# Banded attention: output projection behind the scores, first mask ahead of the residual add, and mask, scale and minimum of a head in one VectorE pass

## The reference

```python
q, k, v = jnp.split(shift_token(x) @ wqkv, 3, axis=-1)      # 8 heads of 64 each
q, k = l2norm(q) * qs, l2norm(k) * ksc
q, k = rotary_xpos(q, k)
...
bq = q.reshape(b, h, w, WINDOW, d) * QK_SCALE               # WINDOW = 64, QK_SCALE = 8
sim = jnp.einsum('bhwid,bhwjd->bhwij', bq, bk)              # own and previous window
mask = (i < j) | (i > j + WINDOW) | (j == -1)
sim = jnp.where(mask, -jnp.finfo(sim.dtype).max, sim)
attn = jax.nn.softmax(sim, axis=-1)
out = jnp.einsum('bhwij,bhwjd->bhwid', attn, bv)
...
x = x + o @ wo
```

## Time and profile before

| | |
|---|---|
| median of 3 runs | 3254.89 us (3253.47 to 3256.94) |
| the profiled execution | 3241.83 us |
| its span, first to last instruction | 3239.8 us |
| mean granted clock of TensorE | 0.893 of full speed |
| busy, share of the span | TensorE 79%, VectorE 60%, ScalarE 48%, GpSimd 25% |
| the four passes, twelve steps of each | 123.2 to 123.5 us each |

### The profile page before, as it was taken

The page is one execution under the profiler, slowest core; times in us unless marked ns, Lnnn a source line. Parts: engine busy times, 40 slices in busy tenths (PEclk is TensorE's granted clock), DMA queues, the critical chain, the costliest instruction groups (busy, mean ns, idle before and its releaser), DMA issues. The chain is left out here.

```text
span 3239.8 us, 44443 instructions
## 1 busy us (share of the span) xinstructions
PE 2552.5 (79%) x15874; PEld 1765.7 (55%) x15874; DVE 1949.3 (60%) x3314; ACT 1567.2 (48%) x3740; POOL 822.1 (25%) x598
## 2 busy tenths in 40 slices
PE   7999987787787778777688888664576888789987
PEld 4555554544543544543577777241242765769877
DVE  5666667747846866756444343335556898475554
ACT  4444446746744764755312121644353765156651
POOL 0000004514502532520235353000000776014500
PEclk9999998989989999998799999787797999687896
DMA  1000001000102000000000000000000222000010
GB/s 38 10 10 10 16 31 39 21 18 16 24 5 66 16 16 20 17 14 18 1 0 0 0 0 0 3 10 7 5 12 28 72 72 93 2 9 1 2 55 14
DMA packets 24921, 63.93 MB, mean 20 GB/s; under 512 B 3217, under 2 KB 9873, under 8 KB 23729
## 3 DMA queue, kind: packets, MB, share of 16 engines
q1 hardware_dynamic: 24752, 61.75, 6.3%
HBM read 44.84 MB, written 1.18 MB: 14 GB/s over the span
## 5 line engine op out<-in xcount | busy, mean ns | idle before, releaser
L796 ACT ACTIVATE window_s<-window_s,window_soft,window_rn 128x128 f32<-128x128 f32 x512 | 246.3, 483 | 41.8 <-DVE window_soft L958 41.6
L866 POOL TENSOR_TENSOR window_s<-window_s,window_soft 128x512 f32<-128x512 f32 x128 | 133.1, 1039 | 340.6 <-DVE window_soft L896 340.2
L874 POOL TENSOR_TENSOR window_pa<-window_pa,window_pb 128x1024 f32<-128x1024 f32 x64 | 151.1, 2361 | 152.2 <-DVE window_pb L941 152.2
L1519 ACT ACTIVATE delta_ym<-ps 128x512 f32<-128x512 f32 x96 | 57.3, 597 | 262.4 <-PE ps L1376 262.4
L674 PE MATMUL ps<-window_of,window_wa 128*128 128x128 f32 x512 | 81.7, 308 | 121.1 <-DVE window_of L892 121.1
L604 PE MATMUL ps<-window_wa,window_sh 128*128 128x512 f32 x256 | 136.0, 658 | 41.4 <-DVE window_pb L941 28.6
L2627 DVE TENSOR_TENSOR_SCAN mamba_bx<-ps,mamba_ab 128x256 f32<-128x256 f32 x256 | 154.7, 667 | 19.1 <-PE ps L2413 18.7
L1687 DVE TENSOR_TENSOR delta_xt<-delta_xt,ps 128x512 f32<-128x512 f32 x96 | 66.1, 688 | 165.2 <-PE ps L1392 145.2
L1575 POOL TENSOR_TENSOR delta_bm<-delta_nt,delta_ct 128x512 f32<-128x512 f32 x112 | 146.9, 1331 | 68.3 <-PE ps L1376 67.5
L948 DVE TENSOR_TENSOR window_s<-ps,window_mask 128x512 f32<-128x512 f32 x128 | 87.8, 686 | 108.6 <-PE ps L641 56.9
L857 POOL MEMSET window_sh<- 64x2048 f32 x2 | 3.6, 1799 | 568.3 <-POOLq L52 568.3
(11 more groups left out here) (572 smaller groups left out, 7017.3 us busy)
## 6 DMA issues: line engine op xcount, KB each, us to landing
mamba_cbr<-mamba_c SPq DMA_DIRECT2D x32, 512.0 KB, 3.7
window_vs<-window_vt SPq DMA_DIRECT2D x64, 128.0 KB, 2.4
switch_w<-in_switch_w SPq DMA_DIRECT2D x4, 2048.0 KB, 10.1
window_wa<-in_window_wa SPq DMA_DIRECT2D x4, 1152.0 KB, 6.8
linattn_wb<-in_linattn_wb SPq DMA_DIRECT2D x6, 513.0 KB, 3.5
window_wb<-in_window_wb SPq DMA_DIRECT2D x4, 537.5 KB, 7.7
window_sh<-y SPq DMA_DIRECT2D x16, 128.0 KB, 2.2
window_sh<-y SPq DMA_DIRECT2D x16, 127.5 KB, 2.4
```

The costliest lines, as they stand in the source:

```text
L796: a = nc.scalar.activation(s[:, k % 2, e, c, :], s[:, k % 2, e, c, :], ACT.Exp, scale=rn[:, k % 4, 0, h:h + 1], bias=soft[:, k % 2, e, 1, ...
L866: nc.gpsimd.tensor_tensor(s[:, k % 2, e], s[:, k % 2, e], soft[:, k % 2, e, 3, :].unsqueeze(2).to_broadcast([P, QC, P]), ALU.mult)\
L874: nc.gpsimd.tensor_tensor(own, own, pb[:, :, :, :].rearrange("p a h d -> p (a h d)"), ALU.add)\
```

## The change

Three edits, all in `window_attention_stage`. (1) TensorE: `project_out` moves from ahead of `project_qk` to behind `scores`. (2) VectorE: the mask of the even heads moves ahead of the residual add `attended`. (3) `mask_and_max` becomes four fused instructions for each group of four heads: (scores + mask) times the negated `rn`, written to `s`, with a running minimum that starts at 3e38 and goes to the bias; a new small instruction `negate` makes the negated factor `nrn` of 128x8 once per tile. `exps` then is exp(-1 * s + bias). The semaphore `masked`, which lets TensorE write the next scores over this bank, is now raised at the end of a group and not after its first instruction.

```diff
@@ TensorE
                     if 2 <= i < TILES + 2:
                         turn_qk(base + i - 2)
-                    if i >= 4:
-                        project_out(base + i - 4)
                     if i < TILES:
                         project_qk(base + i)
                     if 2 <= i < TILES + 2:
                         scores(base + i - 2)
+                    if i >= 4:
+                        project_out(base + i - 4)
@@ ScalarE, inverse
-                    act.wait_ge(st.bias_ready, 2 * (k - 3))
+                    act.wait_ge(st.q_factor, k - 3)
@@ ScalarE, exps
-                act.wait_ge(st.bias_ready, 2 * k + e + 1)
+                act.wait_ge(st.masked, 2 * k + e + 1)
                 for c in range(QC):
                     h = 2 * c + e
                     a = nc.scalar.activation(s[:, k % 2, e, c, :], s[:, k % 2, e, c, :], ACT.Exp,
-                                             scale=rn[:, k % 4, 0, h:h + 1], bias=soft[:, k % 2, e, 1, c:c + 1],
+                                             scale=-1.0, bias=soft[:, k % 2, e, 1, c:c + 1],
                                              accum_out=soft[:, k % 2, e, 2, c:c + 1])
@@ VectorE
+            def negate(k):
+                dve.wait_ge(st.rn_ready, k + 1)
+                if k >= 4:
+                    dve.wait_ge(st.p_ready, 2 * (k - 3))
+                nc.vector.tensor_scalar(nrn[:, k % 4, :], rn[:, k % 4, 0, :], -1.0, None, ALU.mult).then_inc(st.q_factor, 1)
+
             def mask_and_max(k, e):
                 dve.wait_ge(st.sim_ready, k + 1)
                 if k >= 2:
                     dve.wait_ge(st.pt_ready, 2 * (k - 2) + e + 1)
-                nc.vector.tensor_tensor(s[:, k % 2, e], K.ps[:, B_S + e, :].rearrange("p (c n) -> p c n", n=P),
-                                        mask[:, k % 2, :].unsqueeze(1).to_broadcast([P, QC, P]), ALU.add)\
-                    .then_inc(st.masked, 1)
-                dve.wait_ge(st.masked, 2 * k + e + 1)
                 if k >= 2:
                     dve.wait_ge(st.p_scaled, 2 * (k - 2) + e + 1)
-                nc.vector.tensor_reduce(soft[:, k % 2, e, 0, :], s[:, k % 2, e], AX, ALU.max, negate=True)\
-                    .then_inc(st.max_ready, 1)
-                dve.wait_ge(st.max_ready, 2 * k + e + 1)
-                dve.wait_ge(st.rn_ready, k + 1)
-                nc.vector.tensor_tensor(soft[:, k % 2, e, 1, :], soft[:, k % 2, e, 0, :],
-                                        rn[:, k % 4, 0, :].rearrange("p (c a) -> p a c", a=2)[:, e], ALU.mult)\
-                    .then_inc(st.bias_ready, 1)
+                dve.wait_ge(st.q_factor, k + 1)
+                for c in range(QC):
+                    h = 2 * c + e
+                    v = nc.vector.tensor_tensor_reduce(s[:, k % 2, e, c, :], K.ps[:, B_S + e, toks(c, P)], mask[:, k % 2, :],
+                                                       nrn[:, k % 4, h:h + 1], 3e38, ALU.add, ALU.min,
+                                                       accum_out=soft[:, k % 2, e, 1, c:c + 1])
+                v.then_inc(st.masked, 1)
@@ VectorE, the loop
                     if i >= 3:
                         recip(base + i - 3, 1)
+                    if 2 <= i < TILES + 2:
+                        negate(base + i - 2)
+                        mask_and_max(base + i - 2, 0)
                     if i >= 4:
                         attended(base + i - 4)
-                    if 2 <= i < TILES + 2:
-                        mask_and_max(base + i - 2, 0)
                     if i < TILES:
                         cosines(base + i)
```

More of the change, by code:

```diff
@@ L504, in window_attention_stage @@
      st.added, st.k_scaled, st.qk_turned, st.qk_moved, st.v_copied, st.vs0, st.vs1, st.sim_ready, st.masked,
-     st.max_ready, st.bias_ready, st.p_ready, st.recip, st.p_scaled, st.pt_ready, st.pt_copied, st.o_ready, st.o_moved,
+     st.q_factor, st.p_ready, st.recip, st.p_scaled, st.pt_ready, st.pt_copied, st.o_ready, st.o_moved,
      st.proj_ready, st.y_attn, st.t0, st.t1, st.t2, st.t3, st.mean_ready, st.centered, st.square_ready, st.var_ready,
@@ L510, in window_attention_stage @@
         "sined ss_ready ss_safe ss_log rn_ready added k_scaled qk_turned qk_moved v_copied vs0 vs1 sim_ready masked "
-        "max_ready bias_ready p_ready recip p_scaled pt_ready pt_copied o_ready o_moved proj_ready y_attn t0 t1 t2 t3 "
+        "q_factor p_ready recip p_scaled pt_ready pt_copied o_ready o_moved proj_ready y_attn t0 t1 t2 t3 "
         "mean_ready centered square_ready var_ready log_ready rstd_ready scaled norm_ready hid_a hid_g gelu_done "
@@ L537, in window_attention_stage @@
     rn = st.sb("rn", [P, 4, 2, HEADS])
+    nrn = st.sb("nrn", [P, 4, HEADS])
     pa = st.sb("pa", [P, 2, 2, HEADS, DH])
```

## The result

The changed kernel takes 3130.54 us in the median of four runs (3122.68 to 3138.70), the kernel before 3254.18 us on the same chip (3251.76 to 3256.94): a ratio of 0.9623, with a 95% interval from 0.9604 to 0.9643. The forecast was 3174 us, with a range from 3150.

A forecast was written before the change was run, and what follows sets the result against it. A VectorE-TensorE loop of waits was taken as the bound; T = 5.73 + 8p = 8.53 us against 10.15, times 48 intervals, 77.8 us, plus 3 at the ends: 81 us off 3254.9 gives 3174 us. Range 3150 to 3238.

The forecast's parts named there:

- What bounds before: VectorE and TensorE: a loop of waits through the output projection sets 10.15 us per tile; VectorE idles 1.78 us before the mask.
- The new order's 4.41 us: First mask can begin 1.43 + 1.81 + 1.17 = 4.41 us behind the start of the sines, instead of 5.91.
- The pair p: VectorE's fused mask instruction plus accumulator read: 0.26 + 0.09 = 0.35 us, bounded by 0.27 and 0.51.
- the loops next in line: Behind VectorE's 8.53 us per tile: ScalarE's loop at 8.08 us, GpSimd's at 8.44 us, or 8.12 at p = 0.27.
- The slow-clock tile stays slow: One of twelve intervals per pass, 11.61 us at a granted clock of 0.85, was to stay slow.
- rival C: TensorE, busier, gets a lower clock: 3244 us if in every tile, 3209 for half; chance 0.07.
- Fill and drain: Ends of each pass: shorter groups and exponentials save some 0.75 us per pass, 3 us in all, between 0 and 8.
- The split of the sum: The order alone gains 1.35 us per tile (65 us), the mask pass alone in the old order 0.27 us (13 us).
- The side effect on the exponentials: On ScalarE, a constant scale gives 0.39 us steps, 0.72 us back per tile; with 1.92 us kept, the bound is 8.80 us.
- A, the pair holds: On VectorE, the read waits for the main's write: p = 0.51, tile 9.81 us, 3236 us; chance 0.14 including pairs between.
- B, GpSimd blocks the fused instruction: First mask group waits for GpSimd's work: tile 11.3 us, 3311 us; chance 0.09 including any pair above 0.55.
- D: The order does nothing because ScalarE's copies hold the scores; chance 0.04 including no change.

The follow-up runs named there:

- order alone: Kernel before with only the output projection moved behind the scores and the first mask ahead of the residual add, old masks: ratio 1.0025, steady tile 10.18 us.
- transposes first: Changed kernel with odd heads' reciprocal ahead of the norms, transposes of p ahead of the output projection, residual add behind the cosines: 3153.38 us, tile 8.12 us.
- TensorE's order and fused mask: Changed kernel with VectorE's residual add moved back ahead of the first mask: 3288.6 us in one run, steady tile 10.91 us.
- product split, old order: Kernel before with the first group's small product L958 split into four one-column instructions: 3341.05 us in one run.
- fused mask alone: Changed kernel with both order moves undone, keeping fused masks, negation and constant scale: 3179.47 us, ratio 0.9789, steady tile 9.25 us.
- product back: Changed kernel plus one unused 128x4 product of two SBUF tensors behind the first fused group: 3223.2 us, ratio 0.9916, steady tile 9.74 us.
- scale by a pointer: Changed kernel with the exponentials' scale of -1 read from an SBUF column instead of a constant: 3168.15 us, ratio 0.9763, steady tile 8.59 us.
- product split: Kernel before with the new order, old masks and the first group's L958 as four one-column instructions: 3212.2 us, ratio 0.9889, tile 9.30 us.

## Why the prediction was wrong, point by point

**What bounds before** held: order alone took the idle time before the mask from 1.78 to 0.57 us.

**The new order's 4.41 us** was 4.48 (1.45 + 1.86 + 1.17), the cosines 1.09 to 1.14, the residual add 0.20. These terms were right.

**The pair p is the term that was mis-sized.** I took 0.26 + 0.09 = 0.35 us and it was 0.27. That this is just the lower bound was luck: there the main was 0.18 and the read 0.09, while in the runs the read starts with the next main, and a built-in main of the same shape costs 0.26 without any read, so that 0.01 is left for the read. I had given the read a small instruction's step of 0.09 us, which is what ScalarE's read takes and VectorE's does not. By the working's own formula T is then 7.89 us, ScalarE's loop 8.08 and GpSimd's 8.12; measured, 8.03. So the loops next in line were sized to 0.1 us. Which of the three sets the tile was not told apart: VectorE's extra 1.09 us of masks showed in full, ScalarE's extra 0.72 us for 0.56. The pair's worth is 8.53 - 8.02 = 0.51 us, over 48 tiles 24.5 us.

**"The slow-clock tile stays slow"** was the second wrong step. They are gone, 4 x 1.46 us; one tile of 8.78 us at a clock of 1.00 takes 0.75 of it back, so 5 us. That the low clock could follow TensorE's idle time, which the change takes from 2.2 to about 0.25 us a tile, was not asked: rival C looked only for more falls.

**Fill and drain** gave 11.5 us, not 3. From a pass's first cosines to its fourth it is 1.5 us less in each pass (25.21 to 23.66 in the first), 6.2 us in all; from a pass's last cosines to the next pass's first 1.9, 1.6 and 0.2 us less, 3.7 in all. Behind the last cosines of all it is 3.0 us less, and ahead of the very first 1.4 us more (499.70 against 501.07 us from the start of the span); these two, 1.6 together, were not taken apart. I had priced only the groups and exponentials, and took the ends to have little of the detour; but the interval into the fourth cosines alone went from 10.51 to 9.43 us.

So 81 + 24.5 + 5 + 8.5 = 119 us, the difference of the two profiled executions. The pair alone did not bring the time below the range, since with p at 0.27 the prediction has GpSimd's 8.12 us and 3154 us. The 23 us from there to 3130.54 are the 0.09 us by which that loop was sized too long (4), the low-clock tiles (5), fill and drain (8.5), and 5 by which the median lies nearer to the profiled execution than the 13 us that were added.

**The split of the sum failed outright,** though it did not enter the total. The order alone was given 65 us and brought none (1.0025, so 8 us longer); the masks alone 13 us and brought 64; together they bring 124. That the total came out nearer than its two parts was luck. The step that failed is "10.15 to 8.80 us by the order": I moved the mask group 1.5 us earlier and priced its product L958 at its old 0.16 us, with the row of its 1.29 us behind GpSimd in hand. I used that row only to ask what the new instruction would do (rival B) and not what the old one would do at its new place. In the whole change the product is gone, so the total was spared.

**The side effect on the exponentials** was right in size (0.39 against 0.48 us apart) and nearly in weight: 8.59 us with the pointer back, where I had ScalarE's loop at 8.80.

**The rivals.** A, the pair holds: refuted, mains start 0.27 us apart though each lasts 0.34. B, GpSimd blocks the fused instruction: refuted for it, and true for the two-tensor product, and for the negation where it stands beside the sum. C, the clock: did not come in this kernel, but in two neighbours of it, each with TensorE idle for 2.6 to 2.7 us in a tile, and not with TensorE busier. D: its outcome came for order alone, by GpSimd's sum and not by ScalarE's copies.

## What to carry to other kernels

When a step moves, lay each instruction that it carries beside the other engines' work at its new time: a VectorE instruction of 0.1 to 0.2 us, either with two SBUF tensors or with one and a constant, stood for 1.3 to 1.8 us beside a long GpSimd one here, while those with an input in PSUM, the reductions, the reciprocals, and the one-column ones with a scalar per partition were not held. Fusing such an instruction away can be what makes an order worth anything, so price the halves of a change apart and together. Where a change moves TensorE's idle time and the trace has tiles with a low clock, price their going and their coming as well.

## What the runs showed of the hardware that was not expected

The read of VectorE's accumulator, 0.08 us long, starts in the trace together with the next main instruction: a fused one with a read has a step of 0.27 us, a built-in one of the same shape without a read 0.26.

A scale that is a scalar per partition makes a 128x128 exponential 0.49 us long instead of 0.40, and the step 0.48 instead of 0.39.

One-column instructions with a scalar per partition stood 0.12 us apart, where the step was 0.09 for the small ones of the earlier trace rows.

An instruction need not have two SBUF inputs to be held by GpSimd: the negation (128x8, a constant factor) took 1.67 us for its 0.14, and the norms' L913 (128x16, constants) 0.34 for 0.17 in transposes first. The one-column instructions with a scalar per partition, the reciprocals of 128x4 and the reductions of 128x512, also in SBUF throughout, were not held.

The granted clock went with TensorE's longest idle time in a tile. Of the 48 steady intervals of a run it was low in 4 of before (2.2 to 2.3 us idle in most tiles), in 1 of order alone (1.7), in 20 of TensorE's order and fused mask (2.67 in each of these), in 37 of product split, old order (2.5 to 2.7), and in none of the fused mask alone (1.1 to 1.4), product back (1.3), scale by a pointer (0.5) and the changed kernel (about 0.25). In product split, with 1.0 us in most tiles, the single low one is one with 2.08. Yet the first three tiles of product split, old order, had 2.6 to 2.7 us at a clock of 1.00. No run changed the idle time and nothing else, so that it is the cause is argued, not shown; why before falls in just one of twelve stays open.
